# A two-layer conditioned transformer block on one core: the start laid out anew, and the token statistics merged later in a slot

## What is computed

```python
x = layernorm(x) * weight + bias                            # over the 256 features
x = (x + tanh(cond @ lin_w.T + lin_b)) * weight + bias
ada(x, g, b) = (cond @ g.T) * x * rsqrt(mean(x * x) + 1e-6) + cond @ b.T
y = ada(x, attn_gamma_w, attn_beta_w)
q, k, v = y @ W_q.T, y @ W_k.T, y @ W_v.T                   # 16 heads of 16 features
x = x + (cond @ attn_alpha_w.T) * (softmax(q k.T / 4) v @ W_o.T)
y = ada(x, ffn_gamma_w, ffn_beta_w)
h = silu(y @ gate_w.T) * (y @ hidden_w.T)                   # 1024 wide
x = x + (cond @ ffn_alpha_w.T) * (h @ out_w.T + out_b)
```

## Time and profile before

| | |
|---|---|
| runs | 1040.92, 1042.36 and 1042.98 us, median 1042.36 |
| the profiled execution, its own time | 1042.48 us |
| its span in the profile | 1040.7 us (1.8 us lie around it) |
| PE busy | 989.9 us, 95% of the span |
| DVE, ACT, POOL busy | 682.4, 619.2 and 567.3 us |
| TensorE's mean granted clock | 0.988 of full speed |

### The profile page before, as it was taken

How to read it: one execution, slowest core, us unless ns; L and a number is a source line. 1 busy time by engine, 2 the same in 40 slices (tenths; PEclk the granted TensorE clock), 3 DMA queues, 4 the chain that set the end, 5 groups by cost and what they waited for, 6 DMA issues and landing times.

```text
span 1040.7 us, 28677 instructions
## 1 busy us (share of the span) xinstructions
PE 989.9 (95%) x11292; PEld 920.9 (88%) x11292; DVE 682.4 (66%) x1310; ACT 619.2 (59%) x1733; POOL 567.3 (55%) x531
## 2 busy tenths in 40 slices
PE   5777999999999999999999999999999999999997
PEld 4665998999999999999999999999999899999897
DVE  4677666666666666676666667666676766666554
ACT  3456565666566566656656665665666566666432
POOL 3477646566474656647465564746656474443320
PEclk9889999999999999999999999999999999999999
DMA  6010001000100000000000000001000000000000
GB/s 203 2 62 21 2 11 33 11 23 12 32 12 12 32 12 22 12 30 15 12 32 12 22 12 17 27 12 32 12 22 12 12 13 12 12 12 13 11 12 21
DMA packets 20884, 23.37 MB, mean 22 GB/s; under 512 B 1168, under 2 KB 20240, under 8 KB 20752
## 3 DMA queue, kind: packets, MB, share of 16 engines
q1 hardware_dynamic: 20752, 21.54, 6.4%
HBM read 13.15 MB, written 8.39 MB: 21 GB/s over the span
## 4 chain that ended last, share of the span: by engine, by line
PE 68%; DVE 9%; ACT 7%; issue 7%; ACTq 0%; POOLq 0%; POOL 0%; DVEq 0%
PE psum L263 13%; PE psum L265 12%; PE psum L264 12%; PE psum L387 5%; PE psum L453 4%; PE psum L452 4%; PE psum L376 4%; PE psum L451 4%; PE psum L398 3%; ACT probs L778 3%; PE psum L293 1%; PE psum L301 1%; PE psum L306 1%; DVE merge L510 1%; DVE least L547 1%
## 5 line engine op out<-in xcount | busy, mean ns | idle before, releaser
L263 PE MATMUL psum<-xf_hi,ffn_hi 128*128 128x256 f32 x1024 | 287.6, 281 | 3.9 <-DVE normed_f L589 1.6
L264 PE MATMUL psum<-xf_lo,ffn_hi 128*128 128x256 f32 x1024 | 286.2, 280 | 0.0
L265 PE MATMUL psum<-xf_hi,ffn_lo 128*128 128x256 f32 x1024 | 285.6, 279 | 0.0
L778 ACT ACTIVATE probs<-psum,least 128x64 f32<-128x64 f32 x928 | 202.4, 330 | 50.1 <-DVE least L547 26.7
L612 DVE SCALAR_TENSOR_TENSOR late<-tanh,psum 128x512 f32<-128x512 f32 x128 | 88.1, 688 | 207.1 <-ACT tanh L801 206.8
L944 POOL TENSOR_TENSOR probs<-probs,inv_sum 128x512 f32<-128x512 f32 x128 | 141.9, 1109 | 128.3 <-DVE inv_sum L565 127.6
L807 ACT ACTIVATE prod_hi<-late 128x512 fp32r<-128x512 f32 x128 | 80.8, 631 | 210.4 <-DVE late L620 210.4
L263 PEld LDWEIGHTS psum<-xf_hi,ffn_hi 128*128 128x128 f32 x1024 | 192.5, 188 | 5.1 <-issue 3.8
L264 PEld LDWEIGHTS psum<-xf_lo,ffn_hi 128*128 128x128 f32 x1024 | 192.7, 188 | 0.0
L265 PEld LDWEIGHTS psum<-xf_hi,ffn_lo 128*128 128x128 f32 x1024 | 192.6, 188 | 0.0
L626 DVE TENSOR_TENSOR prod_lo<-late,prod_hi 128x512 fp32r<-128x512 f32 x128 | 88.7, 693 | 89.3 <-ACT prod_hi L807 89.3
(11 more groups left out here) (100 smaller groups left out, 2264.0 us busy)
## 6 DMA issues: line engine op xcount, KB each, us to landing
xin<-x_dram SPq DMA_DIRECT2D x16, 512.0 KB, 3.8
out_t_dram<-x_res SPq DMA_DIRECT2D x32, 256.0 KB, 2.1
w_raw<-attn_w_dram SPq DMA_DIRECT2D x1, 1024.0 KB, 7.6
x_res<-gate_w_dram SPq DMA_DIRECT2D x1, 1024.0 KB, 10.4
late<-hidden_w_dram SPq DMA_DIRECT2D x1, 1024.0 KB, 12.1
x_res<-out_w_dram SPq DMA_DIRECT2D x1, 1024.0 KB, 5.6
k_heads<-mod_w_dram SPq DMA_DIRECT2D x1, 448.0 KB, 5.4
ident<-identity_dram SPq DMA_DIRECT2D x1, 64.0 KB, 3.3
```

Of the source, the lines that this page charges most:

```text
L263: pe.matmul(out, stat_hi, mov_hi, start=first, stop=False)
L264: pe.matmul(out, stat_hi, mov_lo, start=False, stop=False)
L265: return pe.matmul(out, stat_lo, mov_hi, start=False, stop=last)
L778: op = act.activation(probs[g % 2][:, h * SEQ:(h + 1) * SEQ], scores[:, h // 2, h % 2], ACT.Exp, bias=least[g % 2][:, h:h + 1], scale=-1.0)
```

## The change

Seven edits.

1. The block's first x comes in two halves of 256 tokens, each with its own statistics, inverse root and normalisation (`load_half`, `half_stats`, `half_rstd`, `normalise_half`). The condition and the first two of the seven modulation matrices are issued ahead of x, the other five behind it (`load_mod`).
2. The first queries and values go to the bank of the down projection (`proj_bank`), so that `queries(0)` no longer waits for `k_out` and `keys(1)` waits for the keys' copy instead of the values' copy. `values(0)` moves from slot -2 to slot 0, behind `score(0)`.
3. For the second part `norm_step` moves the spreading of the inverses, `scale_a` and `apply_beta_a` from slot -2 to -1, and `split_hi_a(1)`, `split_lo_a(1)` from slot -1 to 0. The statistics of block 1 move from slot -5 to -4, behind the residual of part 1.
4. Weight splits: chunks 0 and 1 in slot -4, 2 in -3, 3 in -2, none in -1, then one in each of slots 0 to 7. The load of the output matrix moves from slot 3 to -1.
5. `wide`: up to slot 11 only the even slots have the centring by DVE and the one wide exponential; the odd ones have the eight exponentials on the scores.
6. `token_stats` moves behind `product` in DVE's slot, and `merge_stats` behind it.
7. The small waits follow the new counts.

```diff
-SPLIT_AT = -1
+SPLITS = {-4: (0, 1), -3: (2,), -2: (3,), 0: (4,), 1: (5,), 2: (6,), 3: (7,), 4: (8,), 5: (9,), 6: (10,), 7: (11,)}
+OUT_W_AT = -1
...
         def wide(g):
-            return g < FFN_AT
+            return g < FFN_AT and g % 2 == 0
...
+        def norm_step(s):
+            return 3 if s == -2 else 2 if s == -1 else s % PSEQ
...
+        def proj_bank(w, m):
+            return y_bank if m == 0 and w in (WQ, WV) else work
...
-            load_x(0)
+            sp.dma_start(cond_sb[0:COND, 0:BATCH], cond_t).then_inc(mod_loaded, 16)
+            load_mod(SHIFT, A_BETA, mod_loaded)
+            load_half(0)
             sp.dma_start(ident[:], identity).then_inc(loaded, 16)
             sp.dma_start(vecs[:], feat_vecs).then_inc(loaded, 16)
             sp.dma_start(mask[:], head_mask).then_inc(loaded, 16)
-            sp.dma_start(cond_sb[0:COND, 0:BATCH], cond_t).then_inc(mod_loaded, 16)
-            sp.dma_start(mod_stage[:, 0:7 * D].rearrange("p (w d) -> p w d", d=D),
-                         mod_w.rearrange("w c d -> c w d")).then_inc(mod_loaded, 16)
+            load_half(1)
+            load_mod(A_BETA, F_ALPHA + 1, rest_loaded)
...
-                elif m >= 1:
+                elif m == 2:
                     pe.wait_ge(v_out, m)
+                elif m == 1:
+                    pe.wait_ge(k_out, m)
                 project(WK, m).then_inc(k_mm, 1)
             def queries(m):
-                pe.wait_ge(k_out, m + 1)
+                if m >= 1:
+                    pe.wait_ge(k_out, m + 1)
...
+                if s == 0:
+                    values(0)
                 if j == 0 and is_part(grp + 1):
                     keys(grp + 1)
                 if j == 1 and is_part(grp + 1):
                     queries(grp + 1)
-                if j == 2 and is_part(grp + 1):
+                if s == FIRST_SLOT + 5:
+                    mean_squares(grp)
+                if j == 2 and 1 <= grp + 1 < NPART:
                     values(grp + 1)
...
-            for t in range(TILES):
-                token_stats(0, t)
+            half_stats(0)
...
-            normalise_tokens(0)
+            normalise_half(0, 0, 1)
...
             op.then_inc(shift_made, 1)
+            half_stats(1)
             for s in range(FIRST_SLOT, LAST_SLOT):
...
-                if s == FIRST_SLOT + 3:
+                if s == FIRST_SLOT + 4:
                     for t in range(TILES):
                         token_stats(1, t)
+                    merge_stats(1, 3)
                 if s == FIRST_SLOT + 6:
-                    normalise_tokens(1)
-                if grp % 2 == 0 and 2 <= (grp + 4) // 2 < NBLK:
-                    token_stats((grp + 4) // 2, j)
+                    normalise_half(1, 0, 3)
+                    normalise_half(1, 1, 3)
                 if is_step(f):
                     activate(f)
                 if is_seq(s):
                     invert_sums(s)
                 if is_step(f):
                     product(f)
-                if 0 <= s - SPLIT_AT < WCHUNK:
-                    split_ffn_weights(s - SPLIT_AT)
+                if grp % 2 == 0 and 2 <= (grp + 4) // 2 < NBLK:
+                    token_stats((grp + 4) // 2, j)
+                    if j == 3:
+                        merge_stats((grp + 4) // 2, (grp + 4) // 2 + 2)
+                for c in SPLITS.get(s, ()):
+                    split_ffn_weights(c)
...
+                if s == 0:
+                    split_hi_a(1)
...
-                if j == 3 and is_part(grp + 2):
+                if j == 3 and is_part(grp + 2) and s != -1:
                     split_hi_a(grp + 2)
```

More of the change, by code:

```diff
@@ L558, in invert_sums @@
             def invert_sums(g):
[L559 removed]
+                if wide(g):
+                    dve.wait_ge(exp_made, sum(wide(i) for i in range(g + 1)))
+                else:
+                    dve.wait_ge(scores_read, g + 1)
                 dve.tensor_reduce(row_sum[g % 2][:], probs[g % 2][:].rearrange("p (h k) -> p h k", k=SEQ), AX_X,
```

125 lines of the change are left out of this document (79 added, 46 removed).

## The result

The changed kernel takes 1027.98 us (median; 1026.23 to 1029.87), the one before, run beside it, 1041.64 (1039.45 to 1042.98): a ratio of 0.9871, 95% interval 0.9845 to 0.9897. The forecast was 1029.0. The profiled execution took 1028.54, span 1026.7, so the sum of 13.5 us, made against 1042.48, has to be held against 13.9.

The account below looks back on a forecast made before the run. PE was taken to bound the steady state, a ring of waits with DVE fullest the first slots; 12.5 + 1.3 - 2.0 + 1.7 = 13.5 us less from 1042.48 gave 1029.0 us, 8-in-10 range 1024.0 to 1033.5.

Parts of the forecast that it names:

- The steady state: Merge slot and the one behind it: merge no longer delays the activation, 0.76 + 0.28 = 1.04 a block, 12.5 us less.
- the prediction's upper bound: Steady state: 12.9 us less, if the first merge, whose idle was 1.0 and not 0.67, gives back all of it.
- prod_lo: 1.45 predicted: DVE in merge slots: prod_lo starts 1.45 us behind turn_probs, against 0.88 in the counterpart and 1.99 before.
- the slack: Steady state: prod_lo can come 0.83 us later than in the counterpart slot without lengthening the next slot; 0.55 fits in.
- Rival (c): Steady state: the wait only moves, the slot behind loses what the merge slot gains; 12.5 goes, 1041.5 us; chance 0.04.
- (d): Merge behind the product: its three two-input instructions each wait for POOL, 1.02 us each instead of 0.15; 1046 us; chance 0.02.
- The start: Everything ahead of the steady state: 1.3 less up to the second slot, 2.0 more by slot 8, then 1.7 less.
- second least: Start, up to the second slot: its least moves from 42.40 to 41.1, 1.3 us less; bounds 3 less and 1 more.
- slots 8 to 11: Slots 8 to 10 lose their chunks: slots 8 and 9 give 0.5, slot 10 and slot 11's merge about 1.2; 1.7 less.
- slots 1 to 7: Longer odd-slot exponential chains, late statistics and first merge: slots 1 and 3 +0.8 and +1.4, 2.0 us more at slot 8's start.
- a loss of up to 3: Odd slots with narrow exponentials cost 3 us more, one way to a rival's 1031.5 to 1034 us; that rival's chance 0.15.
- Rival (a): Start gives more: one or two half-clock PE stretches go, 3 to 4 us, chunks give their whole; 1023 to 1026; chance 0.15.

Follow-up runs that it names:

- the run with three more statistics: Changed kernel with three more tile statistics (results unused, in an added tile) between product and merge in the 12 steady-state merge slots: 1044.0 us, one run.
- the run with `values(0)` first: Changed kernel with statistics and merge behind the product only from slot 12 on, and `values(0)` directly behind `score(0)`, ahead of turning x: 1022.07 us.
- all but the merge: Changed kernel with token statistics and merge moved back ahead of the activation: 1038.85 us, ratio 0.997 to the kernel before.

## Why the prediction was right

**The steady state: 12.5 predicted, 13.5 measured.** The mechanism is the one given. Per block the two slots give 15.54 - 14.49 = 1.05 (predicted 1.04); smaller shares, 8.12 to 8.09 and the like, make it 61.03 - 59.95 = 1.08, 13.0 in all. Of the remaining 0.5, 0.36 is a single merge slot of the kernel before, from 271.98 to 280.16: 8.18 us long and not 7.82. It is the wait of 1.0 in the earlier trace rows that the prediction's upper bound allowed for, though it took it for the first merge's and it is the third's; there the activation stood 0.27 us longer, behind an idle time without a releaser:

```profile
279.33 0.69 DVE L612 SCALAR_TENSOR_TENSOR late<-tanh,psum 128x512 f32<-128x512 f32 x1 [0.27 <-issue]
```

The term was a little too small, by this slot and by what moved outside the two slots. The term's parts came as worked out: activation 0.03 after tanh, as predicted; 1.89 ahead of turn_probs (1.87); merge done 1.48 behind it (1.45), with POOL's L1002 ending 0.75 behind it (0.77) and the merge's first row just after. By the rule of the Trainium skill that was weighed there (SBUF — State Buffer, "SBUF: two separate sides"), the trace agrees where two such rows meet: in slot 11 the merge's third row lasts 1.01 instead of 0.15 and ends 0.03 after POOL's L1002. DVE, then POOL:

```profile
95.20 0.15 DVE L540 TENSOR_TENSOR merge<-stats 128x4 f32<-128x4 f32 x1
95.27 1.01 DVE L541 TENSOR_TENSOR merge<-stats 128x4 f32<-128x4 f32 x1
```

```profile
95.20 1.05 POOL L1002 TENSOR_TENSOR probs<-probs,inv_sum 128x512 f32<-128x512 f32 x1
```

**prod_lo: 1.45 predicted, 1.39 measured in eleven of the twelve merge slots.** The twelfth has 1.75, by 0.27 us of idle time between the merge's last row and prod_lo, for which the trace names no releaser. It comes to the end of the slack, and still 7.01 + 7.48 is no longer than the counterpart's 14.50. That the slack is 0.83 was worked out from a single point, and the run with three more statistics bears it out. Rival (c), that the slot behind loses what the merge slot gains, is refuted by 7.48; (d) would have needed three collisions, and there was one of 0.03.

**The start: 1.0 less predicted, 0.5 less in the profile at turn_probs of slot 14 (112.49 and 111.98).** The pieces: modulation matmuls at 4.08, well under the bound of 6.6; first residual at 10.48 (predicted 11.2), since the second half's merge has nothing in its way. The scaling of part 1 came at 29.32 and not at 31.3: the queries no longer wait, and block 1's normalisation took 1.38 us at this place and not the 2.10 of the earlier trace rows. But the keys of part 1 came at 35.56, 0.3 earlier than before and not 0.9 later. The prediction let `values(0)`, xn_hi and these keys hang on the scaling; so they do, but `values(0)` has no need of it. Only turning x has to wait (0.91 us) until the scaling has read its bank, and it stands ahead of `values(0)` on PE. The prediction did not see that this link is one of order alone, and the run with `values(0)` first takes it away and is 5.3 us shorter than the same kernel without it. First least 29.91 (32), second 40.33 (41.1): the second lies in the range of 37.97 to 40.71 that the same instructions give, so its 1 us is no test of the working.

**Slots 1 to 11.** From the second least to slot 12's, slots 1 and 3 were 1.3 and 1.8 longer than before (predicted 0.8 and 1.4), slot 5 0.7 shorter. The runs part these: the narrow exponentials cost the 0.4 that was worked out in either slot, and the late statistics and merge 0.9 in slot 1 and 1.4 in slot 3, where 0.4 and 1.0 was allowed. Slots 8 to 10 gave 15.84 - 13.62 = 2.2 together (predicted 0.5 and part of 1.2), and slot 11 was 1.6 longer (7.78 for 6.2). Only 0.5 of this is the merge's new place, where two of its rows waited for POOL (1.01 and 0.66): with the merge early slot 11 has 7.23, and with the old splits, merge late, 5.88. The rest is what slot 10 gave without its chunk and slot 11 took back. So slots 8 to 11 gave 0.6 and not 1.7; all but the merge gives 2.1 there, and the late statistics and merge take about 1.4 of it. Term by term: second least 2.1 earlier (predicted 1.3), slots 1 to 7 2.2 longer (2.0), slots 8 to 11 0.6 shorter (1.7), steady state 13.5 (12.5), together 14.0 in the spans. Three terms were off by about 1 us each with both signs, so that the sum was off by only 0.5 is partly luck; and as the second least and slot 13 move by some 3 us each with the clock, that the start came so near in this one execution is luck too. Edit 5, for which I feared a loss of up to 3, costs nothing, by its medians and by its slots. Rival (a), that the start gives much more, did not happen for this kernel; the last one, at 1022.07, shows that such a time was there to be had.

## What to carry over

Count what stands on an engine between the instruction that others wait for and the work that nobody waits for, and put the latter behind the last link of the chain; but then measure how late its followers may come, from one slot that was disturbed and one that wasn't: 1.39 against a slack that ends at 1.71 was free, 2.53 cost 0.92 a block. Look at all slots of a kind before one stands for them: the one shown here had 1.75. A reorder that is good in a full steady state can cost time in the start, slot for slot, and that may still not show in the whole, because the clock in one later slot is worth as much. And before an experiment adds a tile, run the tile alone: here it cost as much as the effect that was to be measured.

## What was not expected of the hardware

- **Where tiles lie changes PE's speed.** One unused tile of 864 bytes a partition, and with it all tiles behind it elsewhere, made the feed-forward matmuls up to 1% longer (282 for 279 to 280 ns), others a little shorter, and the kernel 4.2 us longer. The Trainium skill (SBUF — State Buffer, "SBUF: two separate sides") has contention within the engine side only at the pair of ports that VectorE and GpSimd share, and says that PE never waits on anyone; that does not cover this, and the measurement decides. Which tile it is, and whether by its own address or beside another engine's accesses, is open; no run here tells it.
- **The start moves by itself.** The kernel with the unused tile and the changed kernel run the same instructions. Up to the second least they differ by 0.06 us (40.27 and 40.33), though the granted clock between 38.5 and 48.7 us, and with it PE's busy time, is not the same: the changed kernel's row, then that with the tile:

```profile
38.50:48.70 10.20, 8.08 (x90) 7.00 (x86) 6.99 (x13) 6.31 (x19) 3.03 (x4) 0.77 0.00 0
```

```profile
38.50:48.70 10.20, 5.95 (x85) 4.85 (x84) 6.99 (x13) 6.32 (x19) 3.09 (x4) 0.96 0.00 0
```

  There it cost nothing (least of slot 6 at 65.72 and 65.67), as PE had room. Between 100 and 110 us it does: mean clock 0.83 against 1.00, and slot 13, the second with a feed-forward step, takes 9.62 us for 8.08. The two levels are 1.2 and 2.4 GHz. So one profile's total cannot tell parts of the start that are worth a microsecond or two apart; the single slots can, where they repeat.
- **A load's time hangs on its company.** The same 448 KB took 5.4 us from issue to landing behind one load of x and 7.1 behind x in two halves, each in one profile.
